# Decoder block on one core: the weighted sums of self and cross attention issued two steps at a time

## What is computed

```python
x = layernorm(x + attn(x))          # causal self attention, and a second, linear "memory" part
x = layernorm(x + xattn(ctx, ctx, x))
x = layernorm(x + ffn(x))           # gate over 8 experts, the first two have weights
# attn: qk = x @ w_attn.T + b_attn; v = heads(x)
#   y_ar = softmax(causal(q k^T / sqrt(32))) v
#   e = v[1:] - y_ar[:-1];  ma = tril(leaky(q) sigmoid(k2)^T);  y_ma = ma e
#   out = y_ar @ w_proj.T + b + y_ma @ w_proj.T + b
# xattn: softmax(q k^T / sqrt(512)) v with per-head 32x32 weights, then Wo
```

## Time and profile before

| | |
|---|---|
| timed runs, median (lowest to highest) | 1810.16 us (1804.63 to 1816.65) |
| profiled execution: its time, its span | 1812.64 us, 1810.9 us |
| TensorE busy | 1723.4 us, 95% |
| VectorE, GpSimd, ScalarE busy | 70%, 63%, 53% |
| mean granted TensorE clock | 0.978 |

### The profile page before, as it was taken

The page is one execution under the profiler, slowest core; times in us unless marked ns, Lnnn a source line. Parts: engine busy times, 40 slices in busy tenths (PEclk is TensorE's granted clock), DMA queues, the critical chain, the costliest instruction groups (busy, mean ns, idle before and its releaser), DMA issues.

```text
span 1810.9 us, 30473 instructions
## 1 busy us (share of the span) xinstructions
PE 1723.4 (95%) x10474; PEld 1087.7 (60%) x10474; DVE 1267.9 (70%) x2792; ACT 962.3 (53%) x1895; POOL 1133.5 (63%) x933
## 2 busy tenths in 40 slices
PE   6999999999999889999988899999999999999997
PEld 4666666666666457877853356464554646555456
DVE  5677677777777657767856687767768676776744
ACT  4555555555555532433345566565656655565554
POOL 2556556565564644644457776777687677768773
PEclk9999999999999979999988999999999999999999
DMA  6565555555654464666625644434434533443200
GB/s 200 139 160 162 137 156 159 149 162 140 160 151 125 117 204 134 206 187 187 188 75 144 151 100 128 103 105 115 106 104 108 134 95 105 123 106 88 77 24 24
DMA packets 166885, 237.26 MB, mean 131 GB/s; under 512 B 21702, under 2 KB 72902, under 8 KB 166732
## 3 DMA queue, kind: packets, MB, share of 16 engines
q1 hardware_dynamic: 166732, 235.31, 47.1%
HBM read 91.57 MB, written 41.94 MB: 74 GB/s over the span
## 4 chain that ended last, share of the span: by engine, by line
PE 68%; POOL 9%; DVE 7%; DMA 5%; issue 4%; ACT 3%; SPq 3%; POOLq 0%; ACTq 0%; DVEq 0%
PE bank L201 8%; PE bank L1565 8%; PE bank L202 6%; PE bank L203 6%; POOL cross_added L1858 5%; PE bank L351 5%; PE bank L296 4%; PE bank L1449 4%; PE bank L1417 4%; PE bank L1388 4%; PE bank L338 3%; SPq L689 2%; PE bank L1516 2%; DVE cross_negmax L1398 2%; PE bank L1482 2%
## 5 line engine op out<-in xcount | busy, mean ns | idle before, releaser
L1398 DVE TENSOR_REDUCE cross_negmax<-bank 128x1 f32<-128x512 f32 x512 | 339.2, 676 | 161.8 <-PE bank L1388 157.4
L1635 ACT ACTIVATE cpt<-bank 128x512 f32<-128x512 f32 x512 | 295.6, 595 | 147.9 <-PE bank L1417 140.8
L530 DVE CUSTOM_DVE_ANT_0 bank<-bank,future 128x128 f32<-128x128 f32 (+3 forms) x512 | 246.7, 488 | 172.5 <-PE bank L338 171.8
L412 ACT ACTIVATE pt<-bank 128x256 f32<-128x256 f32 (+3 forms) x512 | 224.2, 440 | 257.7 <-PE bank L296 256.8
L1858 POOL TENSOR_TENSOR cross_added<-cross_added,cpt 128x2048 f32<-128x2048 f32 x64 | 292.3, 4568 | 18.8 <-ACT cpt L1635 18.2
L1388 PE MATMUL bank<-cqk 96*128 96x512 f32 x512 | 253.5, 499 | 15.7 <-DVE cross_negmax L1398 13.2
L1417 PE MATMUL bank<-cqk 98*128 98x512 f32 x512 | 226.8, 444 | 13.9 <-ACT cpt L1635 12.7
L594 POOL TENSOR_SCALAR_AFFINE_SELECT pt<-pt 128x512 f32<-128x512 f32 x128 | 81.3, 635 | 252.6 <-ACT pt L412 252.6
L1858 POOL TENSOR_TENSOR cross_added<-cpt,cpt 128x2048 f32<-128x2048 f32 x32 | 146.6, 4580 | 109.6 <-ACT cpt L1635 109.6
L296 PE MATMUL bank<-qk 98*128 98x256 f32 (+2 forms) x512 | 179.8, 355 | 4.7 <-DMA qk<-self_shift 3.6
L201 PE MATMUL bank<-xt_hi,w_hi 128*128 128x512 f32 x384 | 168.1, 438 | 16.8 <-DVE w_lo L488 13.8
(11 more groups left out here) (199 smaller groups left out, 3546.3 us busy)
## 6 DMA issues: line engine op xcount, KB each, us to landing
qk<-stage SPq DMA_DIRECT2D x384, 128.0 KB, 2.3
cqk<-cstage SPq DMA_DIRECT2D x384, 128.0 KB, 2.4
scratch_memory<-memory SPq DMA_DIRECT2D x32, 512.0 KB, 3.9
ma<-scratch_memory SPq DMA_DIRECT2D x32, 512.0 KB, 4.0
raw<-in_x_t SPq DMA_DIRECT2D x32, 256.0 KB, 2.8
v<-in_x SPq DMA_DIRECT2D x32, 256.0 KB, 3.3
scratch_y_ar<-y_ar SPq DMA_DIRECT2D x32, 256.0 KB, 2.2
my_ar<-scratch_y_ar SPq DMA_DIRECT2D x32, 256.0 KB, 4.5
```

What stands on the lines that cost most here:

```text
L412: act.activation(s.pt[step % 3][:, j, 0:SEQ - first], sh.bank[2 + n % 2][:, first - q0:SEQ - q0], ACT.Exp, scale=SCALE_SELF).then_inc(s.ac ...
L530: dve.tensor_tensor_reduce(out=scores, in0=scores, in1=sh.future[:, SEQ - P * (qt + 1):SEQ], scale=-1.0, scalar=-NEG, op0=ALU.add, op1=ALU ...
L1398: dve.reduce_max(s.negmax[gm % 2][:, col:col + 1], max_bank(sh, m)[:, :], AX, negate=True).then_inc(s.dve_max, 1)
L1635: act.activation(s.pt[step % 3][:, j, :], sh.bank[2 + n % 2][:, :], ACT.Exp, scale=SCALE_CROSS).then_inc(s.act_exp, 1)
```

## The change

The weighted sums keep their order and their number; they are issued in pairs. In self, W0 and W1 both in slot 11; W2 and W3 both in slot 4 of the next group, directly before T. In cross, W0 and W1 in slot 12; W2 and W3 in slot 4 of the next group, directly before T. No other engine's list is changed.

```diff
@@ self_tensor
-        if j == 1 and 0 <= n // PER - 2 < NG * TILES:
-            self_weighted(pe, s, sh, n // PER - 2)
+
+        if (kt, j) == (2, 3) and 0 <= g < NG:
+            self_weighted(pe, s, sh, TILES * g)
+            self_weighted(pe, s, sh, TILES * g + 1)
+        if (kt, j) == (1, 0) and 0 <= g - 1 < NG:
+            self_weighted(pe, s, sh, TILES * g - 2)
+            self_weighted(pe, s, sh, TILES * g - 1)
@@ cross_slot_tensor
-    if j == 0 and 0 <= n // PER - 2 < NG * TILES:
-        cross_weighted(pe, second, s, sh, n // PER - 2)
+
+    if j == 0 and kt % 2 == 1:
+        for step in (n // PER - 3, n // PER - 2):
+            if 0 <= step < NG * TILES:
+                cross_weighted(pe, second, s, sh, step)
```

## The result

The changed kernel takes 1819.95 us (median, 1814.63 to 1821.67), the kernel before 1808.05 us (1802.32 to 1818.05) in the same comparison: ratio 1.0057, 95% interval 1.0044 to 1.0070. By the ratio that is 10 us slower (the two medians lie 11.9 apart), within the 1% that the prediction called no change. The profiled execution has a span of 1819.6 us (1810.9 before).

A forecast was written before the change was run, and what follows sets the result against it. TensorE, busy 95% of the span, was taken to bound self attention, with cross mixed. Self +10.4, last groups -1, half clock +2, cross -3, first batch 0 made +8.4 us: 1820 us, range 1795 to 1838.

The forecast's parts named there:

- TensorE's own saving: Joining blocks of weighted sums saves 0.32 us a junction; three junctions save 0.96 to 1.02 us per self group.
- The cover between T and L326: Self: L326 waits 1.33 us for `y_ar` in each group; period 19.40 against 19.03, +10.4 us over 28 groups.
- The last three groups: Self, groups without projections: W3 leaves VectorE's way, about -0.4 us each, -1 in all.
- Half clock in self: Self: a wait of 1.33 us may bring TensorE to half clock; +2 us, bounds 0 and +8.
- Buffer waits: Self and cross: exps of slots 4 and 12 need sums now in those slots; put at nothing, +58 us if uncovered.
- Cross, by group: Cross, full batch: group gains and losses together -1.4 us without the clock, net -0.5 with it, -3 over six batches.
- W0's move: Cross, group 1: W0 was free in slot 8 and is paid in slot 12, +0.5 us.
- The half clock: Cross, group 1: longer idle before slot 11 halves the clock in most batches, 1.2 us a stretch, +0.9 a batch.
- the first batch: Cross, first batch: shorter way from slot 15 to the query, longer idle before slot 12; 0, from -4 to +5 us.
- The upper bound of +6: Cross, six full batches: each pays 1.7 us for the half clock and group 1 the whole 0.87.
- the idle before slot 11: Cross, group 1: with W0 gone from slot 8, TensorE's idle time grows from 1.05 to about 2.2 us.
- Rival A: Whole kernel: TensorE's throughput is all; 96 junctions in self and 64 in cross give -51, 1761 us; chance 0.04.

The follow-up runs named there:

- e16_self9_crossgroups: Against the kernel before: self W0, W1 in slot 9, W2, W3 before T; cross pairs except in the first batch and around each batch's first group; 1777.86 us.
- e17_l326_crossgroups: Against the kernel before: self with the change's pairs and L326 in slot 11 behind W0, W1; cross as in e16_self9_crossgroups; 1773.93 us, ratio 0.9812.
- e2_cross_only: Only the change's cross part, self attention as in the kernel before; 1813.08 us, ratio 1.0018.
- e10_cross_mix: Kernel before with the change's cross pairs, but W0 and W1 apart in the first batch and each batch's first group; 1806.15 us, ratio 0.9986.
- e8_self9_crossmix: Against the kernel before: self W0, W1 in slot 9 and W2, W3, T in slot 4; cross as in e10_cross_mix; 1778.60 us, ratio 0.9835.

## Why the prediction was right

**TensorE's own saving: right.** 0.32 us a junction. Self with all covers kept went from 19.03 to 18.04 (predicted -0.96 to -1.02 for three), group 4 of cross from 30.54 to 29.90 for two, and to 30.22 for one.

**The cover between T and L326: right, and the step that decided the sign.** Predicted L326 at T + 7.73, measured 7.65; from it to the next T 11.67, measured 11.68; period 19.40, measured 19.33 and over 28 groups +7.9 for +10.4. The 0.40 of VectorE's idle went and 0.08 more. That the wait is the cause is shown from both sides: with the pair in slot 9, or with L326 behind the pair, it is gone and the three junctions remain. The last three groups: -0.7 for -1.

**Half clock in self: nothing, where I had +2.** 28 groups took 7.9 us more, and 28 times the steady 0.30 is 8.4: no room for a half-clock term, though each group had 1.18 us of idle. The granted clock over the 28 groups is 1.00, as before.

**Buffer waits at nothing: right.** The exps do wait for the sums now (ScalarE's list of waits, after):

```profile
ACT cpt L1643 <- PE bank L1457: 102.7, 58, 4.6
...
ACT pt L417 <- PE bank L356: 37.8, 31, 1.3
```

But where TensorE is dense, in group 4, both junctions arrived in full (0.64), so none of it reached TensorE there. TensorE's waits for exps in cross did rise by 5.3 us (12.7 to 18.0), but in the full batches these are lost covers and not buffers, and the prediction had no term for them. They are 0.45 and 0.23 in slots 8 and 9 of group 1, where W0 was, with the exp behind ScalarE's gate and normalisation work as before; and 0.72 in group 2 (1.91 in the first full batch), where W2 in slot 0 was, with the exp behind the wait for `ln_shift`.

**Cross, by group.** Group 4 -0.64 and group 2 -0.60 as worked out; in group 2 GpSimd's addition stood at T + 12.01 before (1371.59 less 1359.58) and stands at T + 11.18 now (T at 1371.35), with no wait for the exp:

```profile
1382.53 4.58 POOL L1866 TENSOR_TENSOR cross_added<-cross_added,cpt 128x2048 f32<-128x2048 f32 x1
```

Group 3 -0.24 for -0.32. Group 1 without the clock, worked out from the two runs with one sum moved: W0's move +0.43 (I had +0.5) and W2's junction -0.33 give 28.86. The half clock is the term that was mis-sized: +0.9 a batch, as 1.2 in most; it came in six of six and cost 1.2 to 2.8, mean 1.7 (the mean of group 1, 30.54, less 28.86). So the six full batches of cross gave +2.5 for -3, and the first batch +3.9 for 0, inside its bounds. (The upper bound of +6 for the six was added up wrong: -1.4, 1.7 and 0.4 a batch make +4.) That the idle before slot 11 would grow to 2.2 us in one piece was wrong: the single wait is still 1.06, with 0.45 and 0.23 ahead of it, where the transposed scores wait for ScalarE's exps.

**The sum.** Self came out at +7.2 for +11.4 (its clock term in it), cross at +4.3 for -3, start and memory part at -2.8 for nothing. The errors cancel (8.4 - 4.2 + 7.3 - 2.8 = 8.7), so the total is nearer than its steps were, and that is luck: the -3.5 of the memory part and the 3.9 of the first batch lie in stretches that differ by several us between kernels that do not edit them. Rival A had the right saving and missed the wait; the self part of its saving is what the slot 9 run collects (1780). The Trainium skill, "TensorEngine Tiling (Array Packing)", section "Key Properties", says that a change of tiling mode drains TensorE; the trace agrees with it (0.32 us a junction).

## What to carry to other kernels

Joining blocks of narrow matmuls that stood alone among wide ones saved 0.32 us a junction here, but each block was also work that an in-order engine did while another's chain ran: for each place that a block leaves, list the next wait on that engine and what the block hid. If a wait appears, move the instruction that waits, or the block, by a slot or two; here that turned +0.3% into -1.8%. A gain in one phase says nothing of the same move in the next: slot 9 was worth -1.6% in self, slot 8 cost 1.2% in cross.

## What the runs showed of the hardware that I had not expected

The half clock behind a given idle piece is not settled by the piece. Group 1 of cross has the same wait of 1.03 to 1.07 us ahead of slot 11 in all of these kernels but one, and in its six full batches the slower value (by 1.0 to 2.8 us, with a granted clock of 0.94 or 0.89 for the group where the faster value has 1.00) came once in the kernel before, twice in each of the four runs that edit self alone, three times in `e16_self9_crossgroups`, four times with W2 or W0 moved alone and in `e17_l326_crossgroups`, six times in the change, in `e2_cross_only`, in `e10_cross_mix` and in `e8_self9_crossmix`. Within one run of one program it differs from batch to batch. Only the kernel whose pair in slot 8 filled most of the gap (0.23 left) had it in none, and that one had it in one group 2 and two groups 3. In self, 1.18 us of idle in each of 28 groups left the granted clock at 1.00. What else decides was not found; where a gain hangs on it, only the count over several batches is worth anything.
